# Attention scores and distances as whole-array matmuls with zero-padded key blocks, weighted values of eight heads in one PSUM slot, and maxima sent before the next queries

## The reference

```python
def _stablemax3_s(x):
    pos = 1.0 + x * (1.0 + 0.5 * x * (1.0 + x / 3.0))
    neg = 1.0 / (1.0 - x * (1.0 - 0.5 * x * (1.0 - x / 3.0)))
    return jnp.where(x >= 0, pos, neg)
...
logits = logits - jnp.max(logits, axis=axis, keepdims=True)
s = _stablemax3_s(logits)
return s / jnp.sum(s, axis=axis, keepdims=True)
...
attn = stablemax3(jnp.einsum('bhst,...', q, k) * scale, axis=-1)
out  = jnp.einsum('bhst,bhtd->bhsd', attn, v)
...
h = jax.nn.silu(xf @ w1) * (xf @ w3)          # four experts, F = 512
out = sum over the two chosen experts of gate * (h @ w2)
```

## Time and profile before

| | |
|---|---|
| median of 3 runs | 1258.62 us (1257.82 to 1259.13) |
| the profiled execution | 1257.91 us, of which the span is 1256.2 us |
| busy share of the span | PE 94%, PEld 76%, DVE 82%, ACT 82%, POOL 26% |
| granted TensorE clock, mean | 0.991 |
| DMA | 67.90 MB, mean 54 GB/s |

### The profile page before, as it was taken

The page is one execution under the profiler, slowest core; times in us unless marked ns, Lnnn a source line. Parts: engine busy times, 40 slices in busy tenths (PEclk is TensorE's granted clock), DMA queues, the critical chain, the costliest instruction groups (busy, mean ns, idle before and its releaser), DMA issues.

```text
span 1256.2 us, 29583 instructions
## 1 busy us (share of the span) xinstructions
PE 1180.1 (94%) x10244; PEld 952.3 (76%) x10244; DVE 1034.1 (82%) x2030; ACT 1027.1 (82%) x1102; POOL 328.0 (26%) x706
## 2 busy tenths in 40 slices
PE   2569999999999999999999999999999999999988
PEld 1337777888777788877778877778887777888778
DVE  4876888988888898888888888889888888988833
ACT  2587888888888888889988888898888888888872
POOL 4212333221233222223322222332212233231111
PEclk9988999999999999999999999999999999999999
DMA  5111211121210112211111211111122111111000
GB/s 169 60 61 61 64 34 43 56 64 64 64 61 28 47 54 64 64 64 55 35 43 58 64 64 64 49 41 39 63 64 64 64 43 34 51 64 61 11 5 9
DMA packets 83617, 67.90 MB, mean 54 GB/s; under 512 B 6656, under 2 KB 82048, under 8 KB 83584
## 3 DMA queue, kind: packets, MB, share of 16 engines
q1 hardware_dynamic: 83584, 67.47, 16.9%
HBM read 45.42 MB, written 20.97 MB: 53 GB/s over the span
## 4 chain that ended last, share of the span: by engine, by line
PE 81%; DVE 7%; issue 4%; DMA 4%; ACT 3%; SPq 1%; POOL 0%; DVEq 0%; POOLq 0%; ACTq 0%
PE up_a L757 15%; PE up_b L757 14%; PE up_a L915 10%; PE up_b L915 10%; PE sc L818 9%; PE pv L773 6%; PE sc L898 6%; DMA q_stack<-m_split 3%; PE pv L837 2%; PE misc L850 2%; DVE mx L667 1%; PE misc L873 1%; PE pv L873 1%; DVE xn_T L675 1%; PE misc L955 1%
## 5 line engine op out<-in xcount | busy, mean ns | idle before, releaser
L447 ACT ACTIVATE w_sq<-sc 128x1024 f32<-128x1024 f32 x256 | 262.7, 1027 | 126.8 <-PE sc L818 125.7
L576 DVE SCALAR_TENSOR_TENSOR poly<-w_sq,sc 128x1024 f32<-128x1024 f32 x256 | 310.7, 1214 | 21.0 <-ACT w_sq L447 20.6
L667 DVE TENSOR_REDUCE mx<-sc 128x4 f32<-128x1024 f32 x256 | 304.5, 1213 | 9.8 <-PE sc L898 9.8
L568 DVE TENSOR_TENSOR hid<-silu_a,up_b 128x512 f32<-128x512 f32 x256 | 176.0, 687 | 105.5 <-PE up_b L757 45.8
L488 ACT ACTIVATE poly<-poly,two 128x2048 f32<-128x2048 f32 x128 | 252.1, 1993 | 0.4
L493 ACT ACTIVATE poly<-poly 128x2048 f32<-128x2048 f32 x128 | 243.2, 1901 | 0.0
L470 ACT ACTIVATE silu_a<-up_a 128x512 f32<-128x512 f32 x256 | 153.4, 599 | 56.9 <-PE up_a L757 51.9
L757 PE MATMUL up_a<-xn_hi,w_hi 128*128 128x256 f32 x512 | 167.3, 327 | 1.4 <-ACT silu_a L470 1.4
L366 POOL TENSOR_TENSOR x_resb<-x_res,b_out_all 128x128 f32<-128x128 f32 x64 | 27.8, 456 | 492.9 <-DVE y_acc L638 471.3
L757 PE MATMUL up_b<-xn_hi,w_hi 128*128 128x256 f32 x512 | 154.0, 301 | 0.7 <-DVE y_acc L683 0.5
L773 PE MATMUL pv<-poly,v_pad 128*32 128x256 f32 x2048 | 140.9, 394 | 7.0 <-ACT poly L493 6.6
(11 more groups left out here) (102 smaller groups left out, 1833.5 us busy)
## 6 DMA issues: line engine op xcount, KB each, us to landing
qk_scratch<-qk_split SPq DMA_DIRECT2D x32, 512.0 KB, 2.8
q_stack<-qk_scratch SPq DMA_DIRECT2D x128, 128.0 KB, 2.7
k_stack<-qk_scratch SPq DMA_DIRECT2D x128, 128.0 KB, 2.8
x_in<-in_L_attn_x_dram SPq DMA_DIRECT2D x32, 128.0 KB, 2.1
x_res<-in_L_attn_x_dram SPq DMA_DIRECT2D x32, 128.0 KB, 2.4
out_dram<-y_acc SPq DMA_DIRECT2D x32, 128.0 KB, 1.8
poly<-in_L_ffn_w_dram SPq DMA_DIRECT2D x2, 1024.0 KB, 9.2
q_stack<-m_split SPq DMA_DIRECT2D x64, 16.0 KB
```

The costliest lines, as they stand in the source:

```text
L447: nc.scalar.activation(w_sq[:, u % 2, :], sc[:, u % 2, :], ACT.Square).then_inc(sq_ok, 1)
L568: nc.vector.tensor_tensor(hid[:, 2 * u:2 * u + 2, :].rearrange("p a t -> p (a t)"), silu_a[:, u % 2, :], up_b[:], ALU.mult).then_inc(hid_o ...
L576: nc.vector.scalar_tensor_tensor(poly[:, u, :], w_sq[:, u % 2, :], 3.0, sc[:, u % 2, :], ALU.add, ALU.mult).then_inc(poly_ok, 1)
L667: nc.vector.tensor_reduce(by_row[:, :, 2 * g:2 * g + 2], sc[:, u % 2, :].rearrange("p (j k t) -> p j k t", j=2, k=2), AX.X, ALU.min, negat ...
```

## The change

Four edits:

1. `k_stack` becomes `k_pad` with a block for each j: keys of the heads j in rows 64j to 64j + 59, zeros elsewhere (POOL sets the whole tile to 0 at the start). `q_stack` keeps its rows; the maxima go to rows 124 to 127, and rows 124, 125 (j = 0) or 126, 127 (j = 1) of `k_pad` are ones. `distances` uses all 128 rows with four matmuls of 256 columns. `scores` uses rows 0 to 123, and two heads stand side by side in the moving operand: two matmuls of 512 columns.
2. The keys are loaded with eight DMAs of 64 KB instead of four of 128 KB (12 per batch in all), and twice at the start two more bring the ones.
3. `v_pad` has 48 columns per head (16 zeros, 8 values, a one, 23 zeros). Even groups take columns 16 to 47, odd ones columns 0 to 31, and both add up in the same 32 output rows. So `pv` holds all four groups, one copy (ScalarE, `o_T`) takes it, four transposes after unit 2 replace eight, and VectorE's `normalized` does the division for both query blocks at u = 3, with one reciprocal and two multiplications.
4. `maxima_T` stands before `queries_operand` on PE, and `split_maxima` before `queries_T` on VectorE. `queries_operand` now waits for `m_ok`, since both write the same PSUM bank.

The whole division stands behind polynomial 3 instead of half behind polynomial 2 and half behind polynomial 3. The diff, cut to its core:

```diff
@@ sync
-                    for stack, parts in ((q_stack, (0, 0, 2, 2)), (k_stack, (1, 3, 1, 3))):
-                        for r, part in enumerate(parts):
-                            sp.dma_start(stack[par][r::STEP, :, :].bitcast(F32),
-                                         scratch[part].rearrange("(g e) t -> e g t", g=GP)).then_inc(stacked[par], 16)
+                    for r, part in enumerate((0, 0, 2, 2)):
+                        sp.dma_start(q_stack[par][r::STEP, :, :].bitcast(F32),
+                                     scratch[part].rearrange("(g e) t -> e g t", g=GP)).then_inc(stacked[par], 16)
+                    for r, part in enumerate((1, 3, 1, 3)):
+                        of_head = scratch[part].rearrange("(g j d) t -> j d g t", g=GP, j=2)
+                        for j in range(2):
+                            sp.dma_start(k_pad[par][HALF * j + r:HALF * (j + 1):STEP, :, j, :].bitcast(F32),
+                                         of_head[j]).then_inc(stacked[par], 16)
@@ gpsimd, blank_stacks
-            eng.memset(k_stack[par][:].bitcast(F32), 1.0).then_inc(blank[par], 1)
+            eng.memset(k_pad[par][:].bitcast(F32), 0.0).then_inc(blank[par], 1)
@@ vector
+                def normalized():
+                    m = n - 1
+                    by_head = misc[:].rearrange("p (a j b e) -> p a j b e", a=C * G // 2, j=4, e=16)
+                    dve.wait_ge(oq_full, m + 1)
+                    nc.vector.reciprocal(den_r[:], misc[:].rearrange("p (h e) -> p h e", e=16)[:, :, HD]).then_inc(den_ok, 1)
+                    dve.wait_ge(den_ok, m + 1)
...
+                    for k in range(2):
+                        last = nc.vector.tensor_tensor(
...
+                    last.then_inc(attn_ok, 1)
...
+                    if u == 7 and has(i, off + 1):
+                        split_maxima()
                     if u == 7 and has(i, off + 2):
                         queries_T()
-                    if u == 7 and has(i, off):
-                        dve.wait_ge(pv_full, G * n + 2)
-                        after(dve, oq_full, C * n)
-                        nc.vector.tensor_copy(o_T[:, 0:2, :], pv[:]).then_inc(o_ok0, 1)
-                    if u == 7 and has(i, off + 1):
-                        split_maxima()
@@ tensor, weighted_values
+                first = 16 - 16 * (g % 2)
...
-                        last = nc.tensor.matmul(pv[32 * j:32 * j + 32, g % 2, :], v_pad[par][:, c, 4 * g + j, :],
...
+                        last = nc.tensor.matmul(pv[32 * j:32 * j + 32, g // 2, :],
+                                                v_pad[par][:, c, 4 * g + j, first:first + 32],
+                                                poly[:, C * g + c, at:at + S], start=(g % 2 == 0 and c == 0),
+                                                stop=(g % 2 == 1 and c == C - 1))
@@ tensor, distances
-                        at, rows = (2 * j + k) * S, slice(HALF * j, HALF * j + KROWS)
+                        at = (2 * k + j) * S
                         last = nc.tensor.matmul(sc[:, u % 2, at:at + S],
-                                                k_stack[par][rows, 2 * g + k, c * 128:(c + 1) * 128],
-                                                q_stack[par][rows, 2 * g + k, :], start=True, stop=True)
+                                                k_pad[par][:, 2 * g + k, j, c * 128:(c + 1) * 128],
+                                                q_stack[par][:, 2 * g + k, :], start=True, stop=True)
@@ tensor, scores
-                        for j in range(2):
-                            at, rows = (2 * j + k) * S, slice(HALF * j, HALF * j + MROW)
-                            last = nc.tensor.matmul(sc[:, u % 2, at:at + S],
-                                                    q_stack[par][rows, 2 * g + k, c * 128:(c + 1) * 128],
-                                                    k_stack[par][rows, 2 * g + k, :], start=True, stop=True)
+                        last = nc.tensor.matmul(sc[:, u % 2, 2 * k * S:2 * (k + 1) * S],
+                                                q_stack[par][0:MROW, 2 * g + k, c * 128:(c + 1) * 128],
+                                                k_pad[par][0:MROW, 2 * g + k, :, :], start=True, stop=True)
@@ tensor, queries_operand (now called behind maxima_T and up_a_unit)
                     pe.wait_ge(xn_ok, m + 1)
-                    if has(i, off - 1):
-                        pe.wait_ge(lg_ok, n)
-                    else:
-                        after(pe, qk_out, n + 2)
+                    if has(i, off + 1):
+                        pe.wait_ge(m_ok, n + 2)
```

More of the change, by code:

```diff
@@ L170, in attention_then_experts_kernel @@
         m_ok = sem("m_ok")
+        ones_in = [sem(f"ones_in{i}") for i in range(2)]
         m_stacked = [sem(f"m_stacked{i}") for i in range(2)]
@@ L447, in square @@
                     nc.scalar.activation(w_sq[:, u % 2, :], sc[:, u % 2, :], ACT.Square).then_inc(sq_ok, 1)
[L449 to L480, removed]
@@ new lines, in silu @@
+                def silu(u):
+                    if not has(i, off - 2):
+                        return
+                    k = UP * (n - 2) + u
+                    act.wait_ge(a_full, k + 1)
+                    after(act, hid_ok, k - 1 if u > 1 else k - u)
+                    nc.scalar.activation(silu_a[:, u % 2, :], up_a[:], ACT.Silu).then_inc(silu_ok, 1)
+                silu(0)
+                square(0)
+                if has(i, off - 1):
+                    act.wait_ge(pv_full, G * n)
+                    after(act, oq_full, n - 1)
+                    nc.scalar.copy(o_T[:], pv[:]).then_inc(o_ok, 1)
@@ new lines, in first_half @@
+                square(1)
+                silu(1)
+                square(2)
+                if has(i, off + 1):
+                    m, par = n + 1, (off + 1) % 2
+                    act.wait_ge(v_full, m + 1)
+                    act.wait_ge(consts_v, 4)
+                    after(act, pv_full, G * (m - 1))
+                    for c in range(C):
+                        last = nc.scalar.copy(v_pad[par][:, c, :, 16:16 + HD],
+                                              pv[:, 0, c * D:(c + 1) * D].rearrange("p (h d) -> p h d", d=HD))
+                    last.then_inc(v_ok, 1)
@@ new lines, in first_half @@
+                silu(2)
+                square(3)
+                silu(3)
+                square(4)
+                silu(4)
+                square(5)
+                if has(i, off - 1):
+                    m = n - 1
+                    act.wait_ge(attnT_full, m + 1)
+                    after(act, res_full, m)
+                    nc.scalar.copy(attn_T[:], misc[:, 0:S]).then_inc(attnT_ok, 1)
+                silu(5)
+                square(6)
+                silu(6)
+                silu(7)
@@ new lines, in first_half @@
+                distance(3)
+                ups(3)
+                distance(4)
+                ups(4)
+                distance(5)
+                if has(i, off - 1):
+                    m = n - 1
+                    pe.wait_ge(attn_ok, m + 1)
+                    for c in range(C):
+                        last = nc.tensor.transpose(misc[:, c * 128:(c + 1) * 128], attn[:, c, :], ident[:])
+                    last.then_inc(attnT_full, 1)
+                ups(5)
+                distance(6)
@@ new lines, in first_half @@
+                if has(i, off - 1):
+                    m = n - 1
+                    pe.wait_ge(attnT_ok, m + 1)
+                    for c in range(C):
+                        last = nc.tensor.matmul(misc[:, c * D:(c + 1) * D], attn_T[:, c * 128:(c + 1) * 128],
+                                                proj_T[:, 3, :], start=True, stop=True)
+                    last.then_inc(res_full, 1)
+                ups(6)
+                if has(i, off - 2):
+                    up_a_unit(i, off - 2, 7)
@@ L877, in second_half @@
+                distance(7)
+                if has(i, off - 2):
+                    up_b_unit(i, off - 2, 7)
             def second_half(i, off):
@@ L990, in second_half @@
                     up_a_unit(i, off - 1, 0)
+                if has(i, off + 2):
+                    queries_operand()
                 if has(i, off):
```

163 lines of the change are left out of this document (74 added, 89 removed).

## The result

The changed kernel takes 1264.03 us (median of 6 runs, 1262.67 to 1264.62), the kernel before 1258.67 beside it: ratio 1.0041, 95% interval [1.0028, 1.0054]. It is slower by 5.4 us; 1268 was forecast. The profiled execution has a span of 1261.9 us, 5.7 more than before.

What follows compares the result with a forecast made beforehand. The prediction took PE to bound the first half, DVE and ACT the second. 1257.91 us plus 4 (steady state) plus 7 (start) gave 1269, stated as 1268; forecast 1260 to 1273, wider range 1244 to 1281.

Steps and rivals of the forecast that it cites:

- steady state: Repeating period of 36.7 us: some 0.14 longer, +4 us over 30 batches, bounds -27 to +9.
- (c): End of the last maximum to the next distances(0), 4.45 us before: becomes about 4.5, earlier m_ok offset by next x's transposes.
- the start: First scores of batches 0 to 2, waiting for stacks: +7 us from DMA issue and blanking, bounds 0 and +10.
- What bounds the kernel: Steady period: DVE and ACT set the second half, PE the first; cheaper PE helps only there, as DVE and ACT follow.
- A unit costs 0.48 and is done after 0.64: Distance unit on PE: padded costs 0.48 against 0.62 tiled, gain 0.14, but is done after 0.64 instead of 0.50.
- The loop of two slots: First half: unit start to that of the unit after next takes 4.1 us, overtaking PE's own 3.84 for two units.
- (a): Start of distances(0) to polynomial 7: 18.71 us before, about 18.8 after, waits eating PE's gain of 0.55 to 0.9.
- (b): Polynomial 7 to the end of the last maximum: stays at 13.53 us, DVE all but solid.
- Rival 1: First half keeps half to all of PE's 0.9 per period: 1238 to 1252, sign a period below 36.3; chance 0.28.
- Rival 2: Wait for m_ok and later unit ends cost 0.3 per period and more: 1275 to 1280 with the start; chance 0.16.
- rival 4: Distance units in the first half: two tiles side by side beat their edges, +58, 1325 us; chance 0.02.
- Rival 3: Start costs nothing, small DMAs issuing faster (below 0.4 us for 64 KB), steady state even: 1258 to 1261; chance 0.12.

Runs made afterwards that it cites:

- e4: Changed kernel with scores and distances on PE again as four matmuls on row tiles, maxima and ones in rows 60, 61, 124, 125: 1267.80 us, ratio 1.0074.
- e3: Changed kernel with the division (normalized) behind polynomial 2 (u = 2) instead of polynomial 3: 1255.55 us, ratio 0.9976 to the kernel before.
- e2: Changed kernel with the transposes of the next x and their copy ahead of the maxima again: 1274.77 us, ratio 1.0132.
- e7: Changed kernel with tiles on PE, maxima in the old rows and the old order; one PSUM slot, division at u = 3 and twelve DMAs stay: 1259.81 us.
- e1: Kernel before with only the keys loaded by eight DMAs of 64 KB instead of four of 128 KB per batch: 1261.73 us, ratio 1.0031.
- e11: Kernel before with edit 3 alone (one PSUM slot, one copy, four transposes, one division) and the division at u = 2: 1246.18 us, ratio 0.9913.
- e8: Changed kernel with next x's transposes behind weighted_values(2), projection last on PE, and the last expert sum ahead of xn_T on VectorE: 1262.82 us, ratio 1.0036.
- e10: Changed kernel with e3's and e8's edits, and POOL issuing the first three batches' key DMAs before the second blanking: 1251.62 us, ratio 0.9948.

## Why the prediction was right, step by step

The time came out as forecast, and so did most of the places where PE waits. But the steady state went the other way than forecast (-1.8 instead of +4), and inside (c) and inside the start errors cancelled. That 1264 lies so close to 1268 is in part luck.

- *What bounds the kernel.* Right: a padded unit between first-layer matmuls is 0.16 cheaper for PE, and the period moved by 0.05. In e4 the padding's worth in the period is 0.07.
- *A unit costs 0.48 and is done after 0.64.* Measured 0.46 and 0.64 between first-layer matmuls, and 0.56 or 0.57 for units 0, 1 and 3. So the padding's gain was small even ahead of the waits: at `distances(4)` the changed kernel is 0.23 ahead of e4 (8.26 against 8.49 behind `distances(0)`). The loop of two slots, for which I had 4.1 us from a unit's start to that of the unit after next, took 4.25 from `distances(3)` to `distances(5)` and is what the wait there comes from; elsewhere PE found the slot free. The Trainium skill (TensorEngine Tiling (Array Packing), section Theoretical Speedup) gives two tiles up to twice the speed where a dimension is at most 64. By that rule tiles would have been the better form. The measurement does not agree: e4 and the changed kernel show two tiles level with the padded array here, 36.82 against 36.75.
- *(a) about 18.8.* The places and sizes of the waits were right (0.32 at `distances(5)`, and at the transposes of `attn` 0.37 against four bare steps or 0.27 against e3), but the sum was off by 0.3, and with it the direction: 18.50, less than before. I carried every start with a little too much: `hid` 3 came at +8.64, not +8.8, and `distances(5)` at +10.52, not +10.7 to 10.8. The causes that I gave for the two waits hold: e3 shows the division behind the one at the transposes, e4 the padded unit's later end behind the one at `distances(5)`.
- *(b) stays.* Off by 0.17. Every kernel with 512-column scores has 13.69 or 13.70, every one with tiles 13.53 to 13.55. The forecast took two such scores at 0.44 to 0.48 per unit, cheaper than tiles, and the gain as worth nothing. Measured from 300 to 900 us they take 0.57 on average (0.46 to 0.65) where the tiled ones took 0.40, with a step of 0.11 into them instead of 0.18: no gain, but 0.10 more. VectorE pays for it at two places: the sixth maximum starts 9.31 behind polynomial 7 instead of 9.20, behind an idle time of 0.06, and the router's logits wait 0.24 for PE instead of 0.20.
- *(c) about 4.5 to 4.55, the gain of `m_ok` given back by the next x.* The number was right (4.56), by luck. The forecast's terms, added as they stand, give 622.5 and not 622.3 to 622.4, which would be (c) = 4.7. Two of them were too large: the 1.86 from the projection to `distances(0)` held 0.09 of waiting for the maxima's DMAs that the new order removes, and the 0.1 for more waits did not come; the stretch was 1.68. Nor did I see that the new rows slow the maxima's DMAs by 0.2 to 0.3, which the new order hides (e2, e7), and that in the old rows the new order costs 0.11.
- *The steady state, +4.* It was -1.8. The error per period is -0.31 in the change of (a), +0.17 in (b) and -0.03 in (c), which makes -5 over 30 periods, of the 5.8 that are missing. This is the term that made 1268 of 1264.
- *The start, +7.* Measured 6.7, but of other parts. 2.3 per batch through the DMAs was too much: e1 shows 3.8 for three batches, since batch 0 passes its 2.3 on, batch 1 adds 1.2 and batch 2 only 0.3. The blanking made up 0.95 (first transposes at 11.13 instead of 10.18) where I had 0.8. In batch 0 the stretch from the first scores to the maxima's transposes is 11.60 us instead of 10.77; PE runs slow there in both kernels (the transposes last 0.59, later 0.38; granted clock 0.50 in the changed kernel's trace, though 1.00 stands in that of the kernel before), and with tiles the new order needs only 10.35 (e4). And the new order, which I had as giving 0.3 back in each batch, costs 1.0 (e2). The errors cancelled.
- *Rivals.* Rival 1, with PE's gain kept, did not happen in the kernel as changed. Once the division is moved, (a) is 0.48 (e3) and 0.38 (e11) below before, about half of its 0.9, but the period stays above its sign of 36.3 (36.50, 36.42), and in e11 nothing is padded. Rival 2 and rival 4 are out. Rival 3 fell with the issue time of 0.62.

## What to carry to other kernels

Two heads packed into row tiles and the same heads zero-padded on the whole array came out level here, where a unit is short: 0.62 against 0.46 us of PE between first-layer matmuls, less elsewhere, and in the period 0.07. Look at who waits for the end of a unit, and at the units with other neighbours, not only at what the cheapest one costs the engine. Work merged for fewer instructions moves to one place; put it where its engine idles, which was worth 8.5 us here for one digit. And take a change apart: of four edits one, with its division moved, carried the gain.

## What the runs showed of the hardware

A DMA of 16 KB from 16 partitions took SP 0.55 us to issue into rows 60 and 124 and 0.67 us into rows 124 and 126 (1.10 to 1.13 and 1.34 to 1.36 for two). `distances(0)`, where it waits for two of them, starts 1.58 to 1.61 us after the end of the issue with rows 60, 61, 124 and 125 (before, e1, e7, e11) and 1.66 or 1.67 with rows 124 to 127 (e2, e8, e10), so that the data come about 0.3 later in all. A DMA of 64 KB cost SP 0.62 us to issue, one of 128 KB 0.63. POOL issued eight of 64 KB in 5.15 us. A score matmul of 512 columns started its next 0.31 us later on average, 0.23 at the least, where a first-layer matmul of 256 columns took 0.12.
